# Three SAGE layers over 200,000 sorted edges: where the patch gathers may read, what stays on chip from the last step, and which engine takes which small part

## The reference

```python
h = relu(layernorm(x))                       # x: 6250 x 128
for Wl, bl, Wr in three layers:              # 128 -> 256 -> 256 -> 128
    agg = segment_max(h[src], dst)           # 200,000 edges, sorted by dst
    agg = where(isfinite(agg), agg, 0.0)
    h = leaky_relu(agg @ Wl + bl + h @ Wr, 0.01)
out = x + h
```

## Time and profile before

| | us |
|---|---|
| median of 3 runs (6217.3 to 6219.34) | 6219.27 |
| the profiled execution's own time | 6222.6 |
| its span, first to last instruction | 6220.9 |
| POOL busy, 4861 instructions | 4632.6 |
| DVE busy, 3636 instructions | 2902.1 |
| PE busy, 2258 instructions | 706.5 |
| ACT busy, 675 instructions | 232.1 |

### The profile page before, as it was taken

One profiled execution on the slowest core, in us unless ns is written; L12 is line 12 of the kernel. 1 busy time (PEld: TensorE's weight loads), 2 busy tenths in 40 slices (PEclk: granted clock), 3 DMA queues, 4 the chain that ended last, 5 costly groups with the idle time before them and its releaser, 6 DMA issues. The chain is left out here.

```text
span 6220.9 us, 24572 instructions
## 1 busy us (share of the span) xinstructions
PE 706.5 (11%) x2258; PEld 407.3 (7%) x2258; DVE 2902.1 (47%) x3636; ACT 232.1 (4%) x675; POOL 4632.6 (74%) x4861
## 2 busy tenths in 40 slices
PE   0110011111000680000000000047000000000003
PEld 0000000000000340000000000035000000000002
DVE  5333333333333555555555555565555555555556
ACT  1000000000000110000000000012000000000001
POOL 5777777777777677777777777767777777777776
PEclk8555555555555655555555555565555555555556
DMA  4333333333333576666666666667666666666665
GB/s 131 104 106 106 104 103 105 106 105 104 106 104 103 153 240 210 210 209 212 209 211 209 210 209 209 211 195 252 209 211 209 209 210 209 209 210 211 209 211 166
DMA packets 436613, 1089.93 MB, mean 175 GB/s; under 512 B 101509, under 2 KB 155018, under 8 KB 436586
## 3 DMA queue, kind: packets, MB, share of 16 engines
q0 software_dynamic: 207104, 530.50, 31.0%
q1 hardware_dynamic: 206266, 539.48, 23.2%
q10 hardware_dynamic: 23216, 19.67, 1.0%
HBM read 555.78 MB, written 533.46 MB: 175 GB/s over the span
## 5 line engine op out<-in xcount | busy, mean ns | idle before, releaser
L343 POOL DMA_INDIRECT ring<-features,stage x4692 | 4475.1, 954 | 1491.1 <-issue 1384.2
L638 DVE TENSOR_TENSOR ring<-banks,ring 128x1024 f32<-128x1024 f32 (+1 forms) x1173 | 1226.2, 1045 | 3093.4 <-DMA ring<-features,stage 3076.0
L617 DVE TENSOR_TENSOR banks<-ring,banks 128x1024 f32<-128x1024 f32 (+1 forms) x1173 | 1232.4, 1051 | 37.6
L845 PE MATMUL banks<-ident,ring 128*128 128x128 f32 x20 | 5.0, 428 | 3755.5 <-DVEq L650 3755.5
L827 PE MATMUL banks<-dst_low,own 128*128 128x394 bf16 x200 | 99.2, 496 | 1492.7 <-DVE own L601 1492.7
L845 PEld LDWEIGHTS banks<-ident,ring 128*128 128x128 f32 x20 | 3.9, 222 | 3756.9 <-DVEq L650 3533.0
L811 PE MATMUL banks<-wr,h_turned 128*128 128x256 f32 (+1 forms) x500 | 207.3, 557 | 97.7 <-ACT h_turned L932 97.7
L975 ACT ACTIVATE agg<-zeros 128x512 f32<-128x512 f32 x75 | 47.3, 630 | 3962.2 <-PE banks L876 3962.2
L370 POOL DMA_INDIRECT ring<-running_max_log,end_row x150 | 145.2, 968 | 63.4 <-issue 44.8
L606 DVE COPY stage<-edges 128x8 int32 (+1 forms) x588 | 137.5, 234 | 84.9 <-DVE banks L617 25.8
L813 PE MATMUL banks<-b,ones 1*128 1x256 f32 (+1 forms) x300 | 143.7, 575 | 0.0
(11 more groups left out here) (104 smaller groups left out, 563.7 us busy)
## 6 DMA issues: line engine op xcount, KB each, us to landing
running_max_log<-ring SPq DMA_DIRECT2D x782, 512.0 KB, 3.3
running_max_log<-ring SPq DMA_DIRECT2D x391, 256.0 KB, 2.2
ring<-features,stage POOLq DMA_INDIRECT x4692, 2.8
features<-h_out SPq DMA_DIRECT2D x50, 256.0 KB, 2.3
h_in<-features ACTq DMA_DIRECT2D x100, 128.0 KB
ring<-x SPq DMA_DIRECT2D x5, 640.0 KB, 8.8
features<-ring SPq DMA_DIRECT2D x5, 640.0 KB, 7.2
h_in<-features ACTq DMA_DIRECT2D x50, 64.0 KB
```

What stands on the lines that cost most here:

```text
L343: pool.indirect_dma_start(ring[:, c * w:(c + 1) * w], None, tables[l], bass.IndirectOffsetOnAxis(ap=stage[:, b, u:u + 1].bitcast(U32), axi ...
L617: dve.tensor_tensor(sum_ps[:, 0:CHAINS * w].rearrange("p (h f) -> p h f", h=CHAINS), group(g - 1).rearrange("p (h f) -> p h f", h=CHAINS), ...
L638: dve.tensor_tensor(group(g), sum_ps[:, 0:CHAINS * w], group(g), ALU.max).then_inc(turn, 1)
```

## The change

- The log in DRAM gets a new order of rows: row 0 is the row for nodes with no edges, then the 1512 columns of steps 0 to 26 (`EARLY`), then the 52 of the last step (`LATE_ROWS` onward), then the patch.
- The patch gathers read rows below `LATE_ROWS` only, and POOL issues them without waiting for the last step's stores. That wait moves behind the wait for the patch's store.
- What a run's first node needs from the last step is kept in SBUF: `keep_lead` copies, under a mask, each of its 13 groups into `late_lead`, and DVE merges that into the patch with one more maximum.
- Two more instructions in `end_rows` place an end row in the early or the late part. The joins move from L709 into the node numbers (`alone`); L709 and half of the diagonal matrices (L562) go away.
- POOL issues the loads of dst, src and the words of each run (4 DMAs for the 8 of before), computes the differences of neighbouring dst values, and scales 3 of 10 tiles of h0 in DVE's place; ACT scales 7 where it scaled 8.
- `lane` for the picks is read from a copy in PSUM (`lane_ps`).
- Tile 49, which holds padding alone, is left out of the end gathers, the projections and the stores. The first step of every layer is written out ahead of the loop.

```diff
+    END_TILES = -(-nodes // P)
+    PAIR_TILES = [min(2, END_TILES - 2 * q) for q in range(PAIRS)]
+    EARLY = COLS - LAST
+    NO_EDGES, EARLY_ROWS = 0, 1
+    LATE_ROWS = EARLY_ROWS + P * EARLY
+    PATCHED = LATE_ROWS + P * LAST
...
+        lane_ps = banks[:, 5, BANK - 2 * P:BANK]
...
+            pool.dma_start(dst_runs, dst.rearrange("(h p) j -> p h j", p=P)).then_inc(order_loaded, DMA)
+            pool.wait_ge(const_done, 2)
+                for dest, there in run_neighbours(dst):
+                    pool.dma_start(dest, there).then_inc(order_loaded, DMA)
+            pool.dma_start(src_runs.rearrange("p (h j) -> p h j", h=CHAINS),
+                           src.rearrange("(h p) j -> p h j", p=P)).then_inc(src_loaded, DMA)
+            pool.wait_ge(order_loaded, (LOADS - 1) * DMA)
+            pool.tensor_tensor(rises_runs[:, :, 1:RUN], dst_runs[:, :, 1:RUN], dst_runs[:, :, 0:RUN - 1],
+                               ALU.subtract).then_inc(order_checked, 1)
...
+            for s in range(TAIL_STEPS):
+                share = slice(s * TAIL_TILES + ACT_TILES, (s + 1) * TAIL_TILES)
+                pool.wait_ge(norm_ready, 2 * (s + 1))
+                for k in range(share.start, share.stop):
+                    pool.tensor_scalar(h0_all[:, k, :], x_all[:, k, :], rstd[:, k:k + 1], shift[:, k:k + 1],
+                                       ALU.mult, ALU.add).then_inc(h0_scaled, 1)
+                pool.wait_ge(h0_scaled, (TAIL_TILES - ACT_TILES) * (s + 1))
+                pool.tensor_scalar(h0_all[:, share, :], h0_all[:, share, :], 0.0, None,
+                                   ALU.max).then_inc(h0_rest_done, 1)
...
-                for b in range(BLOCKS):
-                    pool.wait_ge(logged[b], LOGGED[b] * (l + 1))
                 pool.wait_ge(prep_done, PREP)
+                pool.wait_ge(empty_stored, DMA * len(widths))
                 for h in range(CHAINS):
                     pool.indirect_dma_start(
-                        patch[:, h * w:(h + 1) * w], None, logs[w][0:NO_EDGES, :],
+                        patch[:, h * w:(h + 1) * w], None, logs[w][0:LATE_ROWS, :],
                         bass.IndirectOffsetOnAxis(ap=patch_row[:, h:h + 1].bitcast(U32), axis=0),
                     ).then_inc(patch_landed, DMA)
                 pool.wait_ge(patch_stored, DMA * (l + 1))
-                pool.wait_ge(empty_stored, DMA * len(widths))
+                for b in reversed(range(BLOCKS)):
+                    pool.wait_ge(logged[b], LOGGED[b] * (l + 1))
                 pool.wait_ge(ends_step, ENDS)
-                pool.sem_inc(ends_open, 1)
-                for t in range(TILES):
+                for t in range(END_TILES):
...
-                    dve.tensor_tensor(pick_slot(i), lane[:, :].unsqueeze(1).to_broadcast(across),
+                    dve.tensor_tensor(pick_slot(i), lane_ps.unsqueeze(1).to_broadcast(across),
...
+                def keep_lead(g):
+                    dve.wait_ge(lead_kept, KEPT * l + g + 1)
+                    dve.copy_predicated(late_lead[:, 0:CHAINS * w].rearrange("p (h f) -> p h f", h=CHAINS),
+                                        lead_goes_on[:, g, :].unsqueeze(2).to_broadcast([P, CHAINS, w]),
+                                        group(g).rearrange("p (h f) -> p h f", h=CHAINS)).then_inc(lead_kept, 1)
...
+                        if last and g:
+                            keep_lead(g - 1)
...
                         dve.sem_inc(block_scanned, 1)
+                        keep_lead(groups - 1)
...
+                dve.memset(late_lead[:, :], LOWEST).then_inc(lead_kept, 1)
                 scan_step(STEPS - 1, True, False)
...
-                for c in range(kc):
-                    before = sum(s[0] for s in shapes[:l]) // P
-                    dve.wait_ge(join_step, before + c + 1)
-                    dve.tensor_tensor(incoming[:, c, 1:RUNS], carry_scan[:, c, 0:RUNS - 1],
-                                      join_row[:, 0, 1:RUNS], ALU.add).then_inc(incoming_ready, 1)
+                dve.wait_ge(patch_landed, DMA * CHAINS * (l + 1))
+                dve.wait_ge(lead_kept, KEPT * (l + 1))
+                dve.tensor_tensor(patch[:, 0:CHAINS * w], patch[:, 0:CHAINS * w], late_lead[:, 0:CHAINS * w],
+                                  ALU.max).then_inc(lead_joined, 1)
                 dve.wait_ge(incoming_turned, l + 1)
```

More of the change, by code:

```diff
@@ L25 @@
 STORES = 5
-ACT_TILES = 8
+ACT_TILES = 7
 DMA = 16
@@ L33, with gnn_program @@
 TILE_MASK = 0x7FFFFF80
-def gnn_program(nc, x, src, dst, weights, out):
+def gnn_program(nc, x, src, dst, weights, out, nodes):
     NODES, F_IN = x.shape
@@ L529, in _ @@
             dve.tensor_scalar(scratch, dst_t, TILE_MASK, None, ALU.bitwise_and).then_inc(prep_done, 1)
+            dve.tensor_scalar(alone[:, :], joins[:, :], -float(NO_NODE), float(NO_NODE),
+                              ALU.mult, ALU.add).then_inc(prep_done, 1)
             for e in range(2):
@@ L737, in add_own @@
                     dve.wait_ge(z_ready, PAIRS * l + q + 1)
[L738 to L739 removed]
+                    wide = PAIR_TILES[q] * n
+                    dve.tensor_tensor(z_sum[b][:, 0:wide], mm_ps[b][:, 0:wide],
+                                      own[:, q * 2 * n:q * 2 * n + wide], ALU.add).then_inc(sum_done, 1)
                 def leaky(q):
@@ L859, in turn_pair @@
                         pe.wait_ge(agg_done, PAIRS * l + q - 2)
-                    for t in range(2):
+                    for t in range(PAIR_TILES[q]):
                         k = 2 * q + t
@@ L956, in count_run, with keep_pair @@
                                          accum_out=below[:, bass.ds(j * 2 + p, 1)]).then_inc(below_counted, 1)
-                def keep_pair(j, more):
+                def keep_pair(j, loads):
                     if l == 0:
@@ L961, in keep_pair @@
                             count_run(j, p)
-                    for p in range(2):
-                        keep_turned(j, p, more)
+                    for p in range(PAIR_TILES[j] if isinstance(j, int) else 2):
+                        keep_turned(j, p, p < loads)
                         keep_own(j, p)
@@ L984, in _ @@
                 sp.dma_start(x_all[:, t, :], x_rows[:, t, :]).then_inc(x_loaded[s], DMA)
-                if s == 0:
-                    sp.dma_start(dst_runs, dst.rearrange("(h p) j -> p h j", p=P)).then_inc(edges_loaded, DMA)
-            sp.dma_start(src_runs.rearrange("p (h j) -> p h j", h=CHAINS),
-                         src.rearrange("(h p) j -> p h j", p=P)).then_inc(edges_loaded, DMA)
-            sp.wait_ge(const_done, 2)
-            with nc.allow_non_contiguous_dma(reason="one word of each run of edges"):
-                for dest, there in run_neighbours(dst):
-                    sp.dma_start(dest, there).then_inc(edges_loaded, DMA)
             for l, (wl, bl, wr) in enumerate(weights):
@@ L1071 @@
     }
-    out = nc.dram_tensor("out", (rows, arrays["L0_gnn_Wl3"].shape[1]), F32, kind="ExternalOutput").ap()
+    out = nc.dram_tensor("out", (-(-nodes // P) * P, arrays["L0_gnn_Wl3"].shape[1]), F32, kind="ExternalOutput").ap()
     weights = [tuple(given[name] for name in layers[3 * l:3 * l + 3]) for l in range(3)]
-    gnn_program(nc, given["x"], given["src"], given["dst"], weights, out)
+    gnn_program(nc, given["x"], given["src"], given["dst"], weights, out, nodes)
     r = run_bass_kernel_spmd(nc, [arrays], core_ids=[0])
```

283 lines of the change are left out of this document (157 added, 126 removed).

## The result

| | before | after |
|---|---|---|
| median, us (7 runs each, one chip) | 6218.67 (6217.3 to 6219.34) | 6197.03 (6196.26 to 6199.87) |
| ratio of the runs | | 0.9967, 95% interval 0.9956 to 0.9978 |
| profiled execution: time, span | 6222.6, 6220.9 | 6198.77, 6196.9 |
| first gather starts | 40.13 | 63.37 |
| ring gathers of the layers, first start to last | 1993.04, 1953.77, 1954.09 | 1953.76, 1961.05, 1960.60 |

The change is faster, by 21.6 us of medians (0.33%, clear of the interval). The forecast was 46, and 6197 lies above its range of 6157 to 6192. The sign was right and the size was off by half. The table already holds the reason: the first gather starts **23 us later**, where I had said 4 us earlier.

What follows compares the result with a forecast made beforehand. The prediction took POOL's chain of gathers, one each 1.25 us, as the bound. Its terms, -33.7 + 7 - 7.5 - 8 - 4 = -46.2 us, took the median from 6219.3 to 6173; range 6157 to 6192.

Steps and rivals of the forecast that it cites:

- Preparation: Ahead of the first gather: loads, differences and h0 scaling shared out anew start it earlier; -4 us, bounds -6.5 and +6.
- at 40 or later, POOL's small work is the cause: Sign at the first ring gather: expected near 36 us; a start at 40 or later would blame POOL's small work.
- Rival C: Masked copies stall POOL at nearly every gather, or its direct DMAs and small instructions delay h0: 6185 to 6201; chance 0.14.
- Lane table: First layer's picks: reading the table from PSUM ends their stall of POOL's gathers; -33.7 us, bounds 0 and 33.7.
- Leads kept on chip: Each layer's last step: masked copies with two SBUF inputs stall POOL's gathers; +7 us, bounds 0 and +35.
- Patch gathers: Each layer's end: issued without the wait, first end gather 3.9 us earlier in first layer, 3.6 for two wide layers; -7.5.
- Tile 49: Each layer's end: one end gather less (1.25 us) and a last pair halved (some 1.4 us); -8 us over three layers.

Runs made afterwards that it cites:

- e18: The changed kernel with the run words loaded by eight DMAs of one word per row, still from POOL's queue, in place of four: 6177.01 us, ratio 0.9924.
- e7: The changed kernel with only the mask of the masked copies (`lead_goes_on`) moved from SBUF to PSUM: 6187.76 us (one run).
- e14: The changed kernel with the run words in eight DMAs from POOL's queue, the same kernel as e18, on slower chip E: 7000.37 us, ratio 0.9946.

## Why the prediction was wrong, by its own steps

**Preparation, the step that failed.** I took the price of POOL's direct DMAs from L343, "0.95 us per 128 rows", and the joined `prev_last` and `next_first` by their count of rows. That price was for a DMA whose rows are whole; these cut every row into four words of 4 bytes. The joined pair took 5.17 us to issue, POOL stood still for 14.18 us more, and `prev_last` landed 17.6 us after its issue. +23.2 measured at the first gather, in place of -4 and outside the bound of +6. My upper bound had been drawn from POOL's small instructions only, and these are harmless where they come early: in e18 a scaling takes 0.43 us and the differences 2.78, inside the 2 to 6 taken and below the estimate of 3.4. Behind the late loads they stretch to 1.3 us each beside DVE's large instructions, a part of the delay that the loads bring with them. With the words in eight DMAs the step comes out at -5.9 (40.13 to 34.21, on two chips), inside -6.5 to +6. The sign that I had set, "at 40 or later, POOL's small work is the cause", pointed at the wrong half of what POOL got. Rival C did name "POOL's direct DMAs hold h0 back" with 0.14 and a cost up to 28 us above the forecast's 6173, and the measured 6197 lies inside that rival's 6185 to 6201 and above my range's end of 6192: the mechanism was on the list, and the range cut through it.

**Lane table.** Right in mechanism, place and size: 33.7 us, and nothing new late behind it. The rule of the Trainium skill's page SBUF — State Buffer, cited there, is borne out for the picks and for the masked copies: two SBUF inputs stall a gather, one operand moved to PSUM ends it.

**Leads kept on chip.** Right in mechanism, mis-sized: +7 was the sum of 2.9, 2 and 2 (six blocks of 0.3 are 1.8, not 2); the trace has about 0, 7.3 and 6.5, and e7 gets 12.6 back. I had laid the copies beside the gathers at offsets that I chose. In the wide layers DVE's copy and the gathers keep the same phase block after block: five gathers of the third layer begin just behind the copy's start (0.06 us in the row above), which is the dearest place. In the first layer, with copies of 0.73 us, the gathers that begin inside one do so 0.47 to 0.53 us behind its start and take 1.03 us at most. The upper bound of 35 held.

**Patch gathers.** -11.7 for -7.5. First layer: end gather at +11.5 where +12.7 was worked out. Wide layers: the carry scans end at 6121.13, +11.1, where I had +11.7, and from the last maximum's end to the end gather it takes 2.90 us, where I had 3.46.

**Tile 49.** -10.1 for -8, the right terms.

**What came of it.** Forecast sum -46.2, measured -24.0 in the spans; the difference of 22.2 is +27.2 at the start, -3.9 for the collisions that a late start avoids, +9.8 for the copies of the wide layers, and -10.9 for what came out better: the rest of the first chain 1.7, the copies of the first layer 2.9, the patch gathers 4.2, tile 49 2.1.

## What to carry to other kernels

Don't price a DMA by its rows alone, and don't carry the price of one form over to another: merging eight small DMAs into four cost 28 us of start, and a merged one had 127 rows of four single words. 112 rows of four words, or 127 of one, cost nothing of the kind. A stall that two engines' instructions cause each other depends on phase, so bound it by "every block at the dearest place", and remove it by moving one operand (table or mask) to PSUM, which cost DVE nothing here (1213 ns for 1216, 1.28 us for 1.29). When a start moves, look for what it uncovers: 28.7 us earlier gave 24.8.

## What was not expected of the hardware

**Chips differ.** The kernel before takes 6219 to 6224 us on chips A, C and F, and 7013, 7017 and 7042 on D, B and E. The windows of e18 (chip F) and of e14 (chip E), one and the same kernel:

```profile
83.00:1823.00 1740.00, 1316.34 (x1391) 0.53 0.35 106
4300.00:6040.00 1740.00, 1316.23 (x1392) 0.50 0.65 210
```

```profile
83.00:1823.00 1740.00, 1249.41 (x1237) 0.52 0.31 93
4900.00:6640.00 1740.00, 1233.76 (x1229) 0.50 0.58 186
```

(The third layer begins later in e14, so its stretch does too.) In 1740 us of the third layer 1229 gathers in place of 1392, one each 1.42 us, with POOL *less* busy (1234 for 1316 us) and the granted TensorE clock the same. A gather takes 1004 ns in the mean for 946, and POOL idles 0.41 us ahead of one for 0.30, 30 of these 506 us waiting for stores of the log; what holds it for the rest was not tried. The preparation up to the first gather is the same within 1.2 us (34.21 and 35.43).

**A longer stall than the instruction that begins it.** The 4.49-us gather of e18 begins at 40.19, inside L597, and ends at 44.68. That is not 0.79 us behind L597's end (42.84) but 0.13 behind the end of L602 (43.02 to 44.55), the large instruction that follows it, which has one input and a scalar. The kernel before shows the same: the gather of 44.41 begins inside L551 and ends at 48.94, 0.11 behind the end of L555. So an instruction with one input held it too; why this one does is not shown.
